# First dots wait for 41 gathers in place of 44, Pool stopped twice, last tables turned in pairs

## What is computed

```
e = stack([tbl_f[ids[:, f]] for f in 0..25], axis=1)          # 512 x 26 x 128
combined = concatenate([dense[:, None, :], e], axis=1)          # 512 x 27 x 128
inter = einsum('bnd,bmd->bnm', combined, combined)[:, triu]     # 351 pairs
h = concatenate([dense, inter, dense], axis=1)                  # 512 x 607
h = maximum(h @ W_top1 + b_top1, 0)                             # 512
h = maximum(h @ W_top2 + b_top2, 0)                             # 256
y = h @ W_top3                                                  # 512 x 1
```

## Time and profile before

| | |
|---|---|
| Median of three runs | 127.44 us |
| Profiled execution | 127.45 us, span 125.6 us |
| Mean granted TensorE clock | 0.973 |
| TensorE matmul busy | 108.4 us, 86% |
| TensorE weight load busy | 94.9 us, 76% |
| VectorE busy | 84.3 us, 67% |
| ScalarE busy | 78.4 us, 62% |
| Pool busy | 56.3 us, 45% |

### The profile page before, as it was taken

The page is one execution under the profiler, slowest core; times in us unless marked ns, Lnnn a source line. Parts: engine busy times, 40 slices in busy tenths (PEclk is TensorE's granted clock), DMA queues, the critical chain, the costliest instruction groups (busy, mean ns, idle before and its releaser), DMA issues.

```text
span 125.6 us, 2622 instructions
## 1 busy us (share of the span) xinstructions
PE 108.4 (86%) x1036; PEld 94.9 (76%) x1036; DVE 84.3 (67%) x169; ACT 78.4 (62%) x146; POOL 56.3 (45%) x61
## 2 busy tenths in 40 slices
PE   0089998999999999999990599889799997999992
PEld 0065886888888888888880599789689996999890
DVE  5599699999999989977415029969501981385002
ACT  4194929999998997949533029957912693249020
POOL 3377878988788787887786000008700000000000
PEclk9999999999999999999999558999999999999999
DMA  3899999993698998621121000000110000000000
GB/s 73 277 410 398 378 397 393 290 356 84 203 364 197 377 236 310 270 69 46 42 60 44 21 5 0 0 5 23 42 26 5 0 0 5 0 0 8 0 0 1
DMA packets 5582, 17.00 MB, mean 135 GB/s; under 512 B 1473, under 2 KB 1729, under 8 KB 5442
## 3 DMA queue, kind: packets, MB, share of 16 engines
q1 hardware_dynamic: 3890, 13.64, 30.3%
q0 software_dynamic: 1536, 3.15, 9.0%
q10 hardware_dynamic: 144, 0.05, 0.4%
HBM read 16.83 MB, written 0.00 MB: 134 GB/s over the span
## 4 chain that ended last, share of the span: by engine, by line
POOL 39%; PE 26%; issue 19%; DVE 6%; ACT 5%; DMA 3%
POOL rows L329 39%; PE acc_ps L691 10%; PE dots_ps L664 8%; DVE z L347 5%; DMA ids_sb<-ids 3%; ACT z L370 3%; PE turn_ps L705 3%; PE acc_ps L682 2%; PE turn_ps L715 1%; PE acc_ps L715 1%; PE turn_ps L637 1%; ACT cols L370 1%; ACT h L458 1%; DVE h L554 0%; DVE y_sb L559 0%
## 5 line engine op out<-in xcount | busy, mean ns | idle before, releaser
L329 POOL DMA_INDIRECT rows<-tbl,ids_sb x48 | 54.1, 1127 | 17.6 <-issue 13.7
L498 DVE TENSOR_SCALAR onehot<-ids_row,row_number 128x1024 fp32r<-128x1024 int32 x49 | 33.3, 748 | 2.2 <-PE acc_ps L606 1.5
L370 ACT ACTIVATE z<-dots_ps 30x128 f32<-30x128 f32 (+5 forms) x80 | 19.7, 246 | 14.3 <-PE dots_ps L664 13.1
L347 DVE COPY z<-dots_ps 30x128 f32<-30x128 f32 (+5 forms) x80 | 21.0, 263 | 11.1 <-issue 6.9
L664 PE MATMUL dots_ps<-cols 128*64 128x52 f32 x512 | 19.0, 240 | 7.4 <-DMA rows<-tbl,ids_sb 4.4
L664 PEld LDWEIGHTS dots_ps<-cols 128*64 128x64 f32 x512 | 18.2, 157 | 8.6 <-issue 7.5
L596 PE MATMUL acc_ps<-onehot,table_hi 128*128 128x512 f32 x68 | 17.7, 413 | 7.0 <-ACT table_hi L370 7.0
L596 PEld LDWEIGHTS acc_ps<-onehot,table_hi 128*128 128x128 f32 x68 | 13.4, 201 | 10.4 <-issue 6.8
L370 ACT ACTIVATE table_hi<-table_raw 128x1024 fp32r<-128x1024 f32 (+1 forms) x16 | 15.0, 974 | 7.8 <-DMA table_raw<-picked_tables 7.7
L606 PE MATMUL acc_ps<-onehot,table_lo 128*128 128x512 f32 x68 | 17.3, 407 | 0.0
L511 DVE TENSOR_TENSOR table_lo<-table_raw,table_hi 128x1024 fp32r<-128x1024 f32 (+1 forms) x16 | 17.1, 1111 | 0.0
(11 more groups left out here) (43 smaller groups left out, 75.3 us busy)
## 6 DMA issues: line engine op xcount, KB each, us to landing
table_raw<-picked_tables SPq DMA_DIRECT2D x14, 512.0 KB, 7.2
ids_row<-ids_picked SPq DMA_DIRECT2D x7, 512.0 KB, 4.8
table_raw<-w SPq DMA_DIRECT2D x1, 1536.0 KB, 8.4
rows<-tbl,ids_sb POOLq DMA_INDIRECT x48, 4.2
w_sb<-w SPq DMA_DIRECT2D x1, 512.0 KB, 10.7
table_raw<-picked_tables SPq DMA_DIRECT2D x2, 128.0 KB, 4.6
dense_sb<-dense SPq DMA_DIRECT2D x1, 256.0 KB, 9.5
ids_sb<-ids ACTq DMA_DIRECT2D x1, 52.0 KB, 4.3
```

The costliest lines, as they stand in the source:

```text
L329: nc.gpsimd.indirect_dma_start(rows[:, t % GATHER_RING, n, :], None, tables[f][:, :], index).then_inc(rows_in[t][g], 16)
L347: last = copy(z[QUAD * q:QUAD * q + rows_of, t % 2, :, QUAD * s + b0:QUAD * s + b1], src.rearrange("i b c -> i c b"))
L370: return nc.scalar.activation(dst, src, ACT.Copy)
L498: nc.vector.tensor_scalar(onehot[:, c], ids_row[:, pair % IDS_RING], row_number[first_row][:, c:c + 1], None, ALU.is_equal).then_inc(oneho ...
```

## The change

The order of work changes, the arithmetic does not. Tile 0's dots wait for the first 41 gathers (k = 0 to 40). Pool stops before k = 41 until tile 1's dots are done and again before k = 45 until tile 2's dots are done, and tile 2's dots wait for the first 45 gathers. The last group of tile 3 is split into two groups of two tables. Turn (2,2) moves ahead of layer 1 of tile 0, and turns (3,0) and (3,1) move between the two halves of tile 2's dots. Turns (3,2) and (3,3) stand ahead of tile 3's dots. The copies on ScalarE and VectorE are reordered to match. The id load holds 12 columns instead of 26.

```
-GROUPS = [range(s, min(s + 4, len(GATHERED))) for s in range(0, len(GATHERED), 4)]
+GROUPS = [[range(0, 4), range(4, 8), range(8, 12)] if t < TILES - 1 else
+          [range(0, 4), range(4, 8), range(8, 10), range(10, 12)] for t in range(TILES)]
-LATE_GATHER = 44
+LATE_GATHER = 41
-PAUSES = {(3, 2): 1}
-LANDED = {0: [(3, 0), (3, 1)]}
+PAUSES = {41: 1, 45: 2}
+LANDED = {0: 41, 2: 45}
-        ids_sb = sb("ids_sb", [P, TILES, NUM_TABLES], I32)
+        ids_sb = sb("ids_sb", [P, TILES, len(GATHERED)], I32)
...  Pool, ahead of gather k
+                        if k in PAUSES:
+                            pool.wait_ge(dots_done, 2 * (PAUSES[k] + 1))
...  ScalarE
+            move_group(2, 0)
+            move_group(2, 2)
             for t in range(TILES):
-                move_group(t + 2, 0)
                 if t + 1 < TILES:
                     evacuate(t + 1, 0, 0)
                 activate1(t)
-                for g in range(2, NG):
-                    move_group(t + 2, g)
                 if t + 1 < TILES:
                     evacuate(t + 1, 0, 2)
                 activate2(t)
+                if t == 0:
+                    move_group(3, 0)
+                if t == 1:
+                    move_group(3, 2)
...  VectorE
+            move_group(2, 1)
             for t in range(TILES):
                 if t >= 1:
                     move_y(t - 1)
-                move_group(t + 2, 1)
+                if t == 1:
+                    move_group(3, 1)
...
                 activate2(t)
+                if t == 1:
+                    move_group(3, 3)
...  TensorE
+            def landed(count):
+                for t, g in GROUP_AT:
+                    first = t * len(GATHERED) + GROUPS[t][g][0]
+                    if count - 8 < first < count:
+                        pe.wait_ge(rows_in[t][g], 16 * min(len(GROUPS[t][g]), count - first))
...
-                for u, g in LANDED.get(t, ()):
-                    pe.wait_ge(rows_in[u][g], 16 * len(GROUPS[g]))
+                if t in LANDED:
+                    landed(LANDED[t])
...
             dots(1)
-            layer1(0, range(H1_ACT))
-            for g in range(2, NG):
-                turn(2, g)
-            layer1(0, (H1_ACT,))
-            layer2(0)
-            for t in range(1, TILES):
-                if t + 1 < TILES:
-                    dots(t + 1, between=lambda: layer3(t - 1))
-                    turn(t + 2, 0)
-                    turn(t + 2, 1)
-                layer1_dense(t)
+            turn(2, 2)
+            for t in range(TILES):
+                if t >= 1:
+                    layer1_dense(t)
                 if t + 1 == TILES:
                     layer3(t - 1)
                 layer1(t, range(H1_ACT))
-                for g in range(2, NG):
-                    turn(t + 2, g)
                 layer1(t, (H1_ACT,))
                 layer2(t)
+                if t == 0:
+                    def between():
+                        layer3(0)
+                        turn(3, 0)
+                        turn(3, 1)
+                    dots(2, between)
+                if t == 1:
+                    turn(3, 2)
+                    turn(3, 3)
+                    dots(3, lambda: layer3(1))
             layer3(TILES - 1)
```

More of the change, by code:

```diff
@@ L61 @@
 TABLE_RING = 2 * PASS_RING
-GROUPS = [range(s, min(s + 4, len(GATHERED))) for s in range(0, len(GATHERED), 4)]
-NG = len(GROUPS)
+GROUPS = [[range(0, 4), range(4, 8), range(8, 12)] if t < TILES - 1 else
+          [range(0, 4), range(4, 8), range(8, 10), range(10, 12)] for t in range(TILES)]
+FIRST_GROUP = [sum(len(GROUPS[u]) for u in range(t)) for t in range(TILES)]
+GROUP_AT = [(t, g) for t in range(TILES) for g in range(len(GROUPS[t]))]
 GATHER_RING = 3
@@ L142, in mover, with group_number, group_bank @@
     return ["scalar", "scalar", "vector"][g] if t == 0 else ["scalar", "vector"][g % 2]
+def group_number(t, g):
+    return FIRST_GROUP[t] + g
+def group_bank(t, g):
+    return (1 + group_number(t, g)) % 2
 def moved_count(engine, tile, group):
-    return sum(mover(t, g) == engine for t in range(tile + 1) for g in range(NG)
-               if (t, g) <= (tile, group))
+    return sum(mover(t, g) == engine for t, g in GROUP_AT if (t, g) <= (tile, group))
 def pieces_of(t):
@@ L226, in build @@
         table_in = [sem(f"table_in{i}") for i in range(TABLE_RING)]
-        rows_in = [[sem(f"rows_in{t}_{g}") for g in range(NG)] for t in range(TILES)]
+        rows_in = [[sem(f"rows_in{t}_{g}") for g in range(len(GROUPS[t]))] for t in range(TILES)]
         ones_ready = sem("ones_ready")
@@ L313, in _ @@
             for t in range(TILES):
[L314 to L318, removed]
+                for g, group in enumerate(GROUPS[t]):
                     for n in group:
-                        f = GATHERED[n]
                         k = t * len(GATHERED) + n
+                        if t >= GATHER_RING:
+                            old = [g0 for g0, group0 in enumerate(GROUPS[t - GATHER_RING]) if n in group0][0]
+                            pool.wait_ge(turned, group_number(t - GATHER_RING, old) + 1)
+                        if k in PAUSES:
+                            pool.wait_ge(dots_done, 2 * (PAUSES[k] + 1))
+                        if k >= FREE_GATHERS and (k - FREE_GATHERS) % GATHERS_A_PASS == 0:
+                            pool.wait_ge(hi_used, min(4 + (k - FREE_GATHERS) // GATHERS_A_PASS, NP))
                         if k >= LATE_GATHER:
@@ L325, in _ @@
                             nc.gpsimd.memset(breath[:], 0.0).then_inc(breathed, 1)
[L326 to L330, removed]
+                        index = bass.IndirectOffsetOnAxis(ap=ids_sb[:, t, n:n + 1].bitcast(U32), axis=0)
+                        nc.gpsimd.indirect_dma_start(rows[:, t % GATHER_RING, n, :], None,
+                                                     tables[GATHERED[n]][:, :], index).then_inc(rows_in[t][g], 16)
         def move_turned(engine, wait_ge, copy, t, g):
-            if t >= TILES or mover(t, g) != engine:
+            if mover(t, g) != engine:
                 return
-            wait_ge(turned, t * NG + g + 1)
-            n0, n1 = FIRST_GATHERED + GROUPS[g][0], FIRST_GATHERED + GROUPS[g][-1] + 1
-            bank = turn_ps[(1 + t * NG + g) % 2]
+            wait_ge(turned, group_number(t, g) + 1)
+            n0, n1 = FIRST_GATHERED + GROUPS[t][g][0], FIRST_GATHERED + GROUPS[t][g][-1] + 1
+            bank = turn_ps[group_bank(t, g)]
             copy(cols[:, t * P:(t + 1) * P, n0:n1].rearrange("d b n -> d n b"),
@@ L444, in _ @@
             copy(cols[:, P:BATCH, NUM_PICKED - 1], picked_ps(PAIRS - 1)[0][:, P:BATCH]).then_inc(rest_moved, 1)
-            for g in range(NG):
+            for g in range(len(GROUPS[1])):
                 if (1, g) not in PICK_TURNS[NP - 1]:
@@ L632, in turn @@
                 if m >= 2:
[L633 to L637, removed]
+                    engine = mover(*GROUP_AT[m - 2])
+                    pe.wait_ge(turned_moved[engine], moved_count(engine, *GROUP_AT[m - 2]))
+                for i, n in enumerate(GROUPS[t][g]):
+                    last = nc.tensor.transpose(turn_ps[group_bank(t, g)][:, i, :], rows[:, t % GATHER_RING, n, :],
                                                identity[:])
                 last.then_inc(turned, 1)
+            def landed(count):
[3 more added lines that the diff above has]
+                        pe.wait_ge(rows_in[t][g], 16 * min(len(GROUPS[t][g]), count - first))
             def dots(t, between=None):
```

11 lines of the change are left out of this document (4 added, 7 removed).

## The result

The changed kernel takes 122.49 us (median of four, 122.21 to 122.77) against 127.60 us for the kernel before (median of four, 127.31 to 128.08): a ratio of 0.960, 95% interval 0.956 to 0.964. The profiled execution took 122.21 us with a span of 120.4 us, 5.2 us less than before. The forecast was 123.1 us. Medians and ranges in this text hold all executions; ratios with an interval leave out those more than 1.5% above the fastest of their kernel.

A forecast was written before the change was run, and what follows sets the result against it. TensorE was taken as busy nearly throughout, save a 4.4 us wait for gathered rows before tile 0's dots and a clock fall behind it. Terms -3.75 - 1.63 + 1.04 - 0.04 = -4.38 gave 123.1 us, range 122.2 to 126.0.

The forecast's parts named there:

- The start of tile 0's dots: First dots wait for 41 gathers, gather 40 ending last: start at 66.91 in place of 70.66, -3.75 us.
- the smaller id load: Load ahead of all gathers, 52 KB to 24 KB: taken as 0, with -0.67 us as the lower bound.
- The clock: Tile 0's dots: granted clock stays up with the idle time ahead cut to 0.67 us, another -1.63 us.
- The rival in which a turn with a wait behind it lets the clock fall: One clock fall, possibly just ahead of tile 3's dots after the pair turns: 126.0 us, chance 0.10.
- The rule of the Trainium skill on transposes: Full clock does not engage for transposes, so pair turns and a wait could drop it ahead of tile 3's dots.
- The wait for gather 44: Ahead of tile 2's dots: gather 44 ends last, 8.00 us after tile 1's dots in place of 6.96, +1.04 us.
- The second stop and the pairs: Ahead of tile 3's dots: gathers 45 to 47 follow tile 2's dots, pair copies 0.60 us; start 100.17 against 104.55.
- The price of 1.1 us for the turns behind the dots: Turns (3,0), (3,1) inside tile 2's dots cover ScalarE's group copy: price 0, or 1.1 us with that cover gone.
- The sum: Whole kernel: -3.75 - 1.63 + 1.04 - 0.04 = -4.38 us, from 127.44 to 123.1 us.
- the forecast's own span: Whole time from 122.2 us (id load -0.67, shorter landings) to 124.3 us (slower pair copies, later landings).
- The slower rival: Two clock falls, at tile 2's and at tile 3's dots: 128.9 us, chance 0.06.

The follow-up runs named there:

- group 2: Second of three groups of four follow-up kernels, on another chip; the changed kernel itself took 123.86 us there, 0.982 of the kernel before.
- that run: Changed kernel with turns (3,0) and (3,1) behind tile 2's dots, as in the kernel before: 123.01 us, against 122.64 for the changed kernel in its group.
- one stop alone: Changed kernel without the second stop, gathers 41 to 47 in one go behind tile 1's dots: median 125.90 us, against 123.86 for the changed kernel.
- the filled kernel: Kernel before with 17 identity products put into TensorE's idle time ahead of tile 0's dots: 128.61 us, 0.999 of the kernel before.

## Why the prediction was right, step by step

**The start of tile 0's dots.** Forecast 66.91, measured 66.25. The forecast had gather 40 end last; in the run it was TensorE's turns. The term that was mis-sized is that of the smaller id load, put at 0 with a bound of -0.67 where TensorE decides: the bound came true. The id load landed 3.7 us after its issue, not 4.3, and the first gather started 0.52 us sooner, which the smaller load may or may not have done (above). Gather 40 came 1.44 us early (62.60 against 64.04). The rest was picked up on the way: gathers 6 and 7 took 1.0 us less between them, gather 8 gave 0.2 back, and gather 39 took 0.95 us in place of 1.29. None of that was in the forecast, and it was luck that it had the right sign. So is part of the close number: on the chip of group 2 the picking of the same kernel ended later, and its D0 was 67.58. Gathers 6 and 7 before, and VectorE's subtraction beside the first of them:

```profile
13.49 1.97 POOL L329 DMA_INDIRECT rows<-tbl,ids_sb  x1 [0.30 <-issue]
15.77 1.45 POOL L329 DMA_INDIRECT rows<-tbl,ids_sb  x1 [0.31 <-issue]
```
```profile
12.30 2.34 DVE L511 TENSOR_TENSOR table_lo<-table_raw,table_hi 128x1024 fp32r<-128x1024 f32 x2
```

After, the same two gathers, with the subtraction at 12.49 to 14.84, again beside the first alone:

```profile
13.03 1.49 POOL L337 DMA_INDIRECT rows<-tbl,ids_sb  x1 [0.30 <-issue]
14.82 0.94 POOL L337 DMA_INDIRECT rows<-tbl,ids_sb  x1 [0.30 <-issue]
```

Three in four gathers take 0.94 to 1.06 us. Of the 672 in the 14 profiles 200 have such a subtraction beside them at some time, and 101 of these take over 1.2 us; of the other 472 it is 21, gather 7 before among them. The Trainium skill, GPSIMD Engine Reference, section Specifications, has Pool's SBUF interface as shared with VectorE, with contention where a VectorE instruction has two SBUF inputs. The subtraction has two, and these counts agree; they do not explain the 1.45 us of gather 7.

**The clock.** It stayed at 1.00 through waits of 1.78 and 1.25 us, and the term was 1.57 by itself against a forecast of 1.63. The rival in which a turn with a wait behind it lets the clock fall did not happen: ten profiles have four turns and 0.76 to 1.11 us of idle time right ahead of tile 3's dots, and in each these take 2.08 us for a half, the time at full clock. That the term exists to be gained rests on an execution of the kernel before in which the clock falls in full, as it did in the profile (0.973) and did not in all others (see the experiments). The rule of the Trainium skill on transposes (TensorE: Matmul & The Clock Gate, Part 4) would have cost 2.9 us here, by the forecast's working, and these ten rows decide against that.

**The wait for gather 44.** The first memset's distance and the gathers' spacing were right: the fourth gather starts 5.12 us behind the dots of tile 1 (5.13 forecast). It reached TensorE 2.55 us after its start and not 2.87, which is 0.3 us of the error. ScalarE's evacuation was done at 84.86, and tile 2's dots started 0.9 us after it could release them (1.1 forecast).

**The second stop and the pairs.** D2 to D3 was forecast at 13.24 us and took 13.30. The copy of 128x256 took 0.63 us (0.60). The profile has VectorE's copy end last, at 99.21, and ScalarE's at 99.13, as close as worked out. The price of 1.1 us for the turns behind the dots was wrong: that run shows 0.1.

**The sum.** -4.38 forecast, -5.2 measured in both the span and the profiled time. The difference is the earlier start of tile 0's dots (0.66) and the shorter landing of one gather (0.32), less 0.06 each by which the clock gave less and D2 to D3 took more than forecast. Both errors have one sign, and both lie within the forecast's own span.

**What was not foreseen.** The slower rival had two clock falls behind idle time. In the changed kernel none came: the mean clock of its 16 executions is 0.998 to 1.00. The danger lay elsewhere: gathers issued beside dots, which the change avoids. The prediction counted the second stop as a cost and had no price for what it prevents. Nor did it ask in how many executions of the kernel before the clock falls as it did in the one profile.

## What to carry to other kernels

Read an idle gap twice where the clock falls in it: with TensorE kept busy up to the dots, what followed took 1.6 us less. Look at the mean clock of every execution, and not only of the profiled one, before counting such a term in full. Once a wait is removed, look at what had been hidden behind it; here it was the end of the picking stage, which let tile 0's dots start at 65.6 us in one profile and at 68.8 in another. And a stop that costs a microsecond by the profile may be what keeps executions alike (one stop alone: 124.11 to 129.53 us; two: 123.66 to 124.47), so that removing it has to be judged by the spread and not by the best run.

## What the runs showed of the hardware

Where Pool issued gathers beside the small products of the dots, TensorE had gaps that no semaphore explains (five products, then 0.4 us of nothing), 1.7 us in all in one profile and 1.6 in another, with a clock fall behind them; in the same stretch VectorE started an instruction 1.7 and 2.0 us late. A wait of 2.35 us with TensorE idle did not lower the granted clock in one profile (mean 0.999), while 4.4 us did in the kernel before, and in the profile of the filled kernel the clock was at half from 53.25 us on, 1.2 us after TensorE had come back from an idle time of 2.48 us. And the start of the gathers, 0.5 us earlier, became 1.4 us at the 41st, as single gathers took from 0.94 to 1.97 us, the long ones mostly beside a VectorE subtraction.
